# Adding x by an accumulating transfer from memory instead of on GpSimd, in the gated attention kernel

## The reference

```python
x = L0_attn_x
xn = _layernorm(x, axis=-1)
s = _L0_attn_ref(xn, L0_attn_WQ, L0_attn_WK, L0_attn_WV)
g = _silu(_L0_ffn_ref(xn, ...))
x = x + s * g
return x
```

## Time and profile before

| what | us |
|---|---|
| median of three runs | 263.12 |
| lowest and highest of them | 262.28, 264.93 |
| profiled execution, first to last instruction (span) | 260.6 |
| median less span (start and end around the instructions) | 2.5 |
| TensorE busy, 1608 matmuls | 238.8 |
| VectorE busy | 196.4 |
| ScalarE busy | 144.4 |
| GpSimd busy | 66.5 |
| mean granted TensorE clock, share of full speed | 0.977 |

### The profile page before, as it was taken

How to read it: one execution, slowest core, us unless ns; L and a number is a source line. 1 busy time by engine, 2 the same in 40 slices (tenths; PEclk the granted TensorE clock), 3 DMA queues, 4 the chain that set the end, 5 groups by cost and what they waited for, 6 DMA issues and landing times.

```text
span 260.6 us, 5957 instructions
## 1 busy us (share of the span) xinstructions
PE 238.8 (92%) x1608; PEld 210.6 (81%) x1608; DVE 196.4 (75%) x580; ACT 144.4 (55%) x389; POOL 66.5 (26%) x108
## 2 busy tenths in 40 slices
PE   6899989999999999999999999799798979797991
PEld 3788978989999898998999889597777868685751
DVE  2788567988878798877697767867876676879664
ACT  1536746557475564756573386647472818394711
POOL 4223506326081451710110000303030120403032
PEclk9999999999999999999999999979997979999998
DMA  6599924232042401206200000040404022222222
GB/s 181 190 339 295 358 94 163 80 146 62 33 161 80 161 0 74 87 5 241 80 3 1 3 1 0 0 161 0 144 17 151 10 86 75 80 83 80 80 79 82
DMA packets 18924, 25.85 MB, mean 99 GB/s; under 512 B 984, under 2 KB 15840, under 8 KB 18912
## 3 DMA queue, kind: packets, MB, share of 16 engines
q1 hardware_dynamic: 18912, 25.71, 29.1%
HBM read 13.12 MB, written 4.19 MB: 66 GB/s over the span
## 4 chain that ended last, share of the span: by engine, by line
PE 67%; DVE 11%; issue 7%; SPq 6%; DMA 5%; ACT 1%; DVEq 1%; ACTq 0%
PE bank L394 61%; DVE arena L941 4%; DVE arena L1251 4%; DMA xT_lo_all<-arena 3%; PE bank L484 3%; PE bank L444 2%; DMA raw_gate<-in_L_ffn_w_gate 2%; SPq L242 2%; SPq L243 1%; SPq L240 1%; DVE w L1286 1%; DVE w L1267 1%; SPq L230 1%; DVE x_ring L1351 1%; DVE arena L1276 1%
## 5 line engine op out<-in xcount | busy, mean ns | idle before, releaser
L394 PE MATMUL bank<-arena 128*128 128x256 f32 (+3 forms) x560 | 80.9, 294 | 11.3 <-DVE arena L941 9.1
L394 PEld LDWEIGHTS bank<-arena 128*128 128x128 f32 (+1 forms) x560 | 74.6, 193 | 16.3 <-issue 10.2
L394 PE MATMUL bank<-xT_hi_all,arena 128*128 (+4 forms) x256 | 80.8, 371 | 1.1 <-DMA xT_lo_all<-arena 1.1
L941 DVE TENSOR_TENSOR arena<-bank,arena 128x512 fp32r<-128x512 f32 (+5 forms) x99 | 51.5, 535 | 16.0 <-ACT arena L727 15.5
L727 ACT ACTIVATE arena<-bank 128x512 fp32r<-128x512 f32 (+5 forms) x100 | 44.7, 476 | 28.2 <-PE bank L394 26.7
L394 PEld LDWEIGHTS bank<-xT_hi_all,arena 128*128 128x128 f32 x256 | 47.3, 190 | 7.4 <-issue 1.3
L394 PE MATMUL bank<-xT_lo_all,arena 128*128 (+4 forms) x128 | 45.9, 358 | 0.0
L380 POOL TENSOR_TENSOR x_ring<-x_ring,w 128x1024 f32 x7 | 18.3, 2615 | 100.6 <-DVE w L1286 100.6
L394 PE MATMUL bank<-WVG_hi,arena 128*128 128x264 f32 x128 | 30.1, 299 | 0.0
L394 PEld LDWEIGHTS bank<-xT_lo_all,arena 128*128 128x128 f32 x128 | 24.4, 191 | 2.1
L892 ACT ACTIVATE w<-bank 128x512 f32<-128x512 f32 x15 | 9.1, 605 | 30.1 <-PE bank L394 30.1
(11 more groups left out here) (116 smaller groups left out, 331.6 us busy)
## 6 DMA issues: line engine op xcount, KB each, us to landing
x_ring<-in_L_attn_x SPq DMA_DIRECT2D x15, 512.0 KB, 3.6
xT_hi_all<-arena SPq DMA_DIRECT2D x8, 512.0 KB, 2.9
xT_lo_all<-arena SPq DMA_DIRECT2D x8, 512.0 KB, 4.0
out<-x_ring SPq DMA_DIRECT2D x7, 512.0 KB, 2.9
w_sb<-in_L_ffn_w SPq DMA_DIRECT2D x1, 1024.0 KB, 10.4
raw_sw<-in_L_ffn_sw SPq DMA_DIRECT2D x3, 256.0 KB, 4.5
x_ring<-in_L_attn_x SPq DMA_DIRECT2D x2, 256.0 KB, 2.9
raw_qkv<-in_L_attn_WQ SPq DMA_DIRECT2D x1, 256.0 KB, 4.1
```

What stands on the lines that cost most here:

```text
L394: return nc.tensor.matmul(dst, lhsT, rhs, start=start, stop=stop, skip_group_check=True, **kw)
L941: return nc.vector.tensor_tensor(dst, src, high.bitcast(F32), ALU.subtract)
```

## The change

In the second stage, ScalarE writes the gate of sequence i straight into the ring slot i % 2 (`to`), VectorE multiplies it with the attention in the slot, and GpSimd then issues a DMA that reads x of that sequence from memory and adds it to what stands in the slot (`accum_op=ALU.add`). The DMA signals `summed0` or `summed1` with 16. SyncE no longer loads x anew for the middle sequences; it waits for the accumulating DMA, issues the store, and doesn't wait for its landing. That wait moves to ScalarE, which before it writes the gate of sequence i (from i = 2 on) waits until the store of sequence i - 2 has landed (`out_stored0`, `out_stored1`). Sequence 0, the last, is as before: x is loaded by SyncE and added by GpSimd and VectorE from `gate`. The loops of the second stage on GpSimd, SyncE and ScalarE are written out in Python. The diff also changes the list of semaphore names (left out).

```diff
--- before.py
+++ after.py
...
@@ -247,33 +247,25 @@
             copy_xT(B - 1)
 
 
-            def reload_x(i):
-                sp.wait_ge(s["x_loaded"], 16 * (B + i - 1))
-                load_x(sequence(i), i)
-
-            sp.wait_ge(s["xn_done"], B)
-            reload_x(0)
-            reload_x(1)
-
             def store(i):
-                sp.wait_ge(s["summed"], i + 1)
-                sp.dma_start(out_v[sequence(i), :, :, :], x_ring[:, i % 2, :, :]).then_inc(s["out_stored"], 16)
-                sp.wait_ge(s["out_stored"], 16 * (i + 1))
-
-            with sp.Fori(0, B - 3) as i:
+                sp.wait_ge(s[f"summed{i % 2}"], 16 * (i // 2 + 1))
+                sp.dma_start(out_v[sequence(i), :, :, :], x_ring[:, i % 2, :, :]).then_inc(s[f"out_stored{i % 2}"], 16)
+
+            for i in range(B - 2):
                 store(i)
-                reload_x(i + 2)
-            store(B - 3)
-            reload_x(B - 1)
+
+            sp.wait_ge(s["out_stored1"], 16 * (B // 2 - 1))
+            load_x(sequence(B - 1), B - 1)
             store(B - 2)
 
             for n in (1, 0, 2):
                 tiles = LAST_PIECES[n]
                 if n == 0:
-                    sp.wait_ge(s["summed"], B)
+                    sp.wait_ge(s["last_added"], 1)
                 else:
                     sp.wait_ge(s["last_summed"], n)
                 sp.dma_start(out_v[0, :, tiles, :], x_ring[:, (B - 1) % 2, tiles, :]).then_inc(s["last_stored"], 16)
+            sp.wait_ge(s["out_stored0"], 16 * (B // 2))
             sp.wait_ge(s["last_stored"], 16 * len(LAST_PIECES))
 
 
@@ -374,18 +366,16 @@
 
 
             def add_x(i):
-                pool.wait_ge(s["x_loaded"], 16 * (B + i))
                 pool.wait_ge(s["gated"], 2 * (i + 1))
-                slot = x_ring[:, i % 2, :, :]
-                nc.gpsimd.tensor_tensor(slot, slot, gate[:, :, :], ALU.add).then_inc(s["summed"], 1)
-
-            with pool.Fori(0, B - 1) as i:
+                pool.dma_start(x_ring[:, i % 2, :, :], x_v[sequence(i), :, :, :], accum_op=ALU.add).then_inc(s[f"summed{i % 2}"], 16)
+
+            for i in range(B - 1):
                 add_x(i)
 
-            pool.wait_ge(s["x_loaded"], 16 * (2 * B - 1))
+            pool.wait_ge(s["x_loaded"], 16 * B)
             pool.wait_ge(s["last_gated"], 1)
             slot = x_ring[:, (B - 1) % 2, LAST_PIECES[0], :]
-            nc.gpsimd.tensor_tensor(slot, slot, gate[:, LAST_PIECES[0], :], ALU.add).then_inc(s["summed"], 1)
+            nc.gpsimd.tensor_tensor(slot, slot, gate[:, LAST_PIECES[0], :], ALU.add).then_inc(s["last_added"], 1)
 
 
         @block.tensor
@@ -887,9 +877,12 @@
 
             def silu_out(i, half):
                 act.wait_ge(s["o_done"], 2 * i + half + 1)
-                if not isinstance(i, int) or i > 0:
-                    act.wait_ge(s["summed"], i)
-                nc.scalar.activation(gate[:, 2 * half:2 * half + 2, :].rearrange("p t d -> p (t d)"), o_bank[:, :],
+                if isinstance(i, int) and i < 2:
+                    act.wait_ge(s["xn_done"], B - 1 + i)
+                elif i < B - 1:
+                    act.wait_ge(s[f"out_stored{i % 2}"], 16 * (i // 2))
+                to = gate if i == B - 1 else x_ring[:, i % 2, :, :]
+                nc.scalar.activation(to[:, 2 * half:2 * half + 2, :].rearrange("p t d -> p (t d)"), o_bank[:, :],
                                      ACT.Silu).then_inc(s["gate_done"], 1)
 
             silu_hidden(0, 0)
@@ -913,7 +906,7 @@
                 h_high(i, 1)
                 rows_high(i, 1)
 
-            with act.Fori(1, B - 1) as i:
+            for i in range(1, B - 1):
                 step2(i)
             i = B - 1
             silu_hidden(i, 0)
@@ -1282,7 +1275,7 @@
             def gate_attn(i, half):
                 dve.wait_ge(s["gate_done"], 2 * i + half + 1)
                 b = sequence(i)
-                g2 = gate[:, 2 * half:2 * half + 2, :]
+                g2 = x_ring[:, i % 2, 2 * half:2 * half + 2, :]
                 return nc.vector.tensor_tensor(g2, g2, attn_all[:, bass.ds(b * T + 2 * half, 2), :], ALU.mult)
 
             pair_one_hots(0, 0)
@@ -1334,7 +1327,7 @@
             gate_attn(i - 1, 1).then_inc(s["gated"], 1)
             h_low(i, 0)
             h_low(i, 1)
-            dve.wait_ge(s["x_loaded"], 16 * (2 * B - 1))
+            dve.wait_ge(s["x_loaded"], 16 * B)
             def times_attn(n):
 
                 tiles = LAST_PIECES[n]
```

More of the change, by code:

```diff
@@ L181, in build @@
         sum_w, pair_out = raw_flat[:, 0:H], raw_flat[:, H:H + PAIRS]
-        names = """x0_half0 x0_half1 w_loaded x_loaded out_stored last_stored experts_loaded
+        names = """x0_half0 x0_half1 w_loaded x_loaded out_stored0 out_stored1 last_stored experts_loaded
             const_part const_ready wq_turned wq_ready wk_ready m_summed m_hi_ready m_ready wvg_hi wvg_ready gate_turned
@@ L190, in build @@
             route logits_max shifted route_exp inv_sum scored counted rows_ready
-            h1_done h3_done h_silu_done h_mult_done h_hi h_lo o_done gate_done gated summed
+            h1_done h3_done h_silu_done h_mult_done h_hi h_lo o_done gate_done gated summed0 summed1
             bc_done one_hot_done gathered rows_silu rows_hi rows_lo pair_one_hot_done accumulated0 accumulated1
-            inv_part wqk_loaded sum_ready sum_turned pairs_ready last_tile_done last_gate_done last_gated last_summed bias_loaded""".split()
+            inv_part wqk_loaded sum_ready sum_turned pairs_ready last_tile_done last_gate_done last_gated last_added last_summed bias_loaded""".split()
         s = {n: sem(n) for n in names}
```

## The result

The changed kernel takes 246.44 us in the median (245.09 to 248.34), the kernel before 263.34 us measured beside it; the ratio is 0.938, with a 95% interval of 0.933 to 0.943. The profiled execution has a span of 243.4 us, 17.2 less than before, at a mean granted clock of 0.995. In some executions of a kernel the granted clock is lower and the time one or two per cent longer; the medians here are of all executions, the ratios are of the others alone.

A forecast was written before the change was run, and what follows sets the result against it. TensorE was taken to bound the second stage, its waits for VectorE lying on the path. 8.75 + 1.89 + 0.34 + 4.67 = 15.65 us off 263.1 gave 247.5 us, range 245.0 to 255.0.

The forecast's parts named there:

- The waits for `h_low` and `one_hot`: Second stage: TensorE's waits for VectorE go once GpSimd's additions leave; five of 1.75 us (8.75) and one of 1.89.
- The clock: Second stage: three windows with the granted clock falling to 0.50 after a wait return to full clock, saving 4.67 us.
- The first rival: Second stage: the clock falls anyway without the waits, so 4.67 us are not regained; 252.1 us, chance 0.15.
- The step: One second-stage loop step: 12.77 less the 1.75 us wait makes 11.02 us, with TensorE still the bound.
- 5 x 1.75: Second stage: five TensorE waits for `h_low`, one per step, of 1.75 us each, saving 8.75 us.
- The end: From the sixth addition on: the `one_hot` wait of 1.89 us goes, and the seventh addition's block saves 0.34 us.
- The accumulating transfer: GpSimd's DMA adding x into the ring slot: 6.5 us to landing, a load plus a store, costing 0 us.
- the cover of 11.3: Second-stage ring: the accumulating transfer may take up to 11.3 us before `silu_out` two steps later waits; cost 0.
- the sum of the formula: Ring cycle over two steps: 7.4 + L + 3.3 us, L the transfer's latency; ScalarE waits if over 22.
- The rival of the issue: GpSimd's DMA issue stops VectorE as the addition did, while descriptors are written; 256 us, chance 0.08.
- the formula and its 0.88: Second-stage step: a blocking GpSimd instruction of d us makes TensorE wait d - 0.88 us.
- Around the span: Whole kernel: the median stands 2.5 us above the profiled span, kept and added to the forecast span of 245.0.

The follow-up runs named there:

- e1: Kernel before with only the second stage's loops on GpSimd, SyncE and ScalarE written out in Python: 263.02 us, ratio 0.998.
- e3: Changed kernel plus a GpSimd multiplication of 1024 unused elements per partition, same input twice, ahead of each of the first six accumulating transfers: 256.48 us.
- e5: Changed kernel plus a GpSimd multiplication of 512 elements ahead of each of the first six accumulating transfers: 250.5 us in a single run.
- e9: Changed kernel plus a GpSimd multiplication of 1024 elements with two different inputs ahead of each of the first six accumulating transfers: 264.65 us, ratio 1.011.
- e4: Changed kernel plus a GpSimd memset (only writes) of 1024 elements per partition ahead of each of the first six accumulating transfers: 249.95 us, single run.
- e10: The changed kernel again, unaltered, timed as the measure for another run on the same chip: 248.93 us, ratio to the kernel before 0.934.
- e6: Changed kernel with each accumulating transfer done twice, the second after the first lands, to double the latency: 255.8 us in a single run.

## Why the prediction was right

The forecast was 247.5 us in a range of 245.0 to 255.0; measured were 246.44.

- **The waits for `h_low` and `one_hot`.** 8.75 + 1.89 us were to go, and no such wait is left. e1 excludes the loops; e3, e5 and e9 bring the waits back by the length of GpSimd's instruction alone.
- **The clock.** 4.67 us were to come back; the second stage's steps are at 1.00. e9 shows the connection: the falls return with waits of 1.75 us, and none stood in the steps of e3 with 1.26. From 150 to 230 us the granted clock is 1.00 in the changed kernel and in all nine other traces in which TensorE doesn't wait 1.75 us for VectorE, and below it in the three in which it does (before, e1, e9). The first rival, that the clock falls anyway, is out for the steps. But the prediction tied the falls to the waits alone, and for the kernel as a whole that is too simple: at the passage between the stages the clock fell in e4 and e10 behind a pause of only 0.35 us, and in the changed kernel's trace it didn't.
- **The step, 11.02 forecast, 10.82 measured.** The term that was mis-sized is "5 x 1.75". The idle time that the trace shows ahead of `shared_out` begins at the modelled end of the four short matmuls before it, 0.40 us after their start; without a wait the next matmul starts 0.21 us after them (199.63 and 199.84). Each wait thus cost 0.2 us more than its row says: 12.77 - 10.82 = 1.95 for a row of 1.75, and the same 0.2 in e3 and e5. Over five steps that is 1.0 us.
- **The end.** 1.89 + 0.34 = 2.2 us were forecast from the sixth addition on. From 234.44 to the span's end it was 26.2 us before, and from 219.87 it is 23.5 now: 2.6 us. The forecast is 0.4 short.
- **The accumulating transfer.** The estimate of 6.5 us was 5.9. At 5.9 us no wait for it appears, as the cover of 11.3 said; e6 shows that waits come at 12 to 13 us and confirms the sum of the formula, while its two terms were off by 1.1 us each, in opposite directions. The store of the seventh sequence is issued at 238.22, still ahead of the last pieces at 239.94:

```profile
238.22 0.38 SPq L252 DMA_DIRECT2D out<-x_ring  x1
239.94 1.39 SPq L267 DMA_DIRECT2D out<-x_ring  x3
```

- **The rival of the issue.** GpSimd's issue takes 1.27 us and stops nothing. The Trainium skill, page "SBUF — State Buffer" (section "Who interferes with whom"), has the block on GpSimd instructions that read SBUF and not on those that only write. The trace agrees with both halves: `pair_one_hots` lasts 2.12 us beside a multiplication of 2.26 (e3) and 0.42 beside a memset of 0.96 (e4), and 0.42 beside an issue of 1.27 in the changed kernel. With the formula and its 0.88 an issue that did block would have cost 0.4 us per step, which no step shows.
- **Around the span, and luck.** The sum put the span at 245.0 us, and it is 243.4, 1.6 too high: 1.0 for the steps, 0.4 for the end and 0.2 ahead of the first step. To this the prediction added 2.5 us, as the median less the span. The profiled execution has 1.8 us around its span (245.17 less 243.4), and the median is 3.0 above that span, because two of the four executions took 248 us. That the forecast came within 1.1 us of the median and not 1.6 is luck of this kind. The mechanisms were right, and the sum was 1.6 us short of the gain.

## What to carry to other kernels

When one instruction's maximum is many times its median on the same sizes, look for what ran on the other engine at that moment: here a GpSimd instruction of 2.6 us that nobody waited for held VectorE, and through it the path, for its whole length. Before moving the work elsewhere, try to start it where VectorE's next instructions have slack, or where they don't read two inputs from SBUF; one moved line gave most of what the rewrite gave. And a removed pause of the matrix engine may be worth more than its length, when a fall of the clock follows it.

## What the runs showed of the hardware

A memset on GpSimd beside a two-input instruction of VectorE costs VectorE nothing (0.42 us, e4), while a multiplication of the same size costs it nearly the multiplication's own length (2.12 us beside 2.26, e3). A multiplication of 1024 elements with one and the same input twice takes 2.26 us on GpSimd, with two different ones 2.76 us. An accumulating transfer of 512 KB lands in 5.9 us, about 2.4 us more than a load. Five pauses of TensorE of 1.26 us, one in each step, had no fall of the clock behind them (e3); of the five of 1.75 us three had one in the kernel before and in e9, and two in e1, where a third fall came behind the one of 1.89 us. A single pause of 1.75 us in e6 had none, and in e4 and e10 the clock fell behind one of 0.35 us, after which it stood at 0.50 for some 6 us.
